# Convolution bias moved to VectorE, first expert pairs loaded earlier, a fill moved among the pairs

## The reference, cut to what matters

```python
x = x + _L0_conv_ref(_ln_c(x), ...)          # gating, 3x3 attention, product with gus, 1x1 product
t = t + _L0_ffn_ref(_ln_t(t), ...)           # 8 experts, each token goes to its best 2
x = x + _L1_conv_ref(_ln_c(x), codebook, bias)   # depthwise 7x7, out + bias[None, :, None, None]
t = t + _L1_ffn_ref(_ln_t(t), ...)           # 8 experts, best 2, with a capacity per expert
```

## Time and profile before

| | us |
|---|---|
| median of 3 runs | 2272.59 |
| lowest, highest | 2270.89, 2274.28 |
| the profiled execution's own time | 2273.36 |
| its span, first to last instruction | 2271.6 |
| TensorE busy | 1646.8 (72%) |
| VectorE busy | 1095.9 (48%) |
| GpSimd busy | 1023.3 (45%) |
| ScalarE busy | 697.3 (31%) |
| DMA, mean over the span | 122 GB/s |

### The profile page before, as it was taken

How to read it: one execution, slowest core, us unless ns; L and a number is a source line. 1 busy time by engine, 2 the same in 40 slices (tenths; PEclk the granted TensorE clock), 3 DMA queues, 4 the chain that set the end, 5 groups by cost and what they waited for, 6 DMA issues and landing times.

```text
span 2271.6 us, 34896 instructions
## 1 busy us (share of the span) xinstructions
PE 1646.8 (72%) x9963; PEld 1386.0 (61%) x9963; DVE 1095.9 (48%) x4024; ACT 697.3 (31%) x1433; POOL 1023.3 (45%) x1041
## 2 busy tenths in 40 slices
PE   4899996998559999999999908870000029999944
PEld 3777775776549999899988808870000016666632
DVE  3465557655555445677678872285000002222257
ACT  0323322232124444555555511030000014444412
POOL 2000004442357777767544470017777745554520
PEclk9999998999779999999999958985555559999965
DMA  3165544653866665998789445601110012232258
GB/s 114 49 113 77 103 90 98 140 104 74 131 149 179 182 181 166 232 240 233 201 211 234 149 107 113 125 21 51 55 51 25 4 25 77 80 88 77 79 190 272
DMA packets 325342, 277.62 MB, mean 122 GB/s; under 512 B 72514, under 2 KB 301655, under 8 KB 325051
## 3 DMA queue, kind: packets, MB, share of 16 engines
q1 hardware_dynamic: 259898, 207.65, 38.6%
q0 software_dynamic: 31488, 55.94, 7.6%
q10 hardware_dynamic: 33792, 12.06, 2.0%
HBM read 167.37 MB, written 109.43 MB: 122 GB/s over the span
## 4 chain that ended last, share of the span: by engine, by line
PE 54%; DMA 15%; DVE 13%; issue 7%; POOL 6%; ACT 3%; SPq 1%; DVEq 1%; POOLq 0%; ACTq 0%
PE zp L708 8%; DMA slots_cap<-arena 7%; PE tp L865 7%; PE zp L984 6%; POOL slots_cap L596 5%; PE tp L875 4%; PE gp L887 3%; PE zp L887 3%; PE tp L997 3%; DMA out<-arena 3%; PE tp L790 2%; PE zp L875 2%; PE gp L805 2%; DMA slots<-arena 2%; DVE arena L1674 2%
## 5 line engine op out<-in xcount | busy, mean ns | idle before, releaser
L596 POOL DMA_INDIRECT slots<-arena x256 | 252.9, 988 | 550.7 <-DVE arena L1459 376.8
L636 POOL DMA_INDIRECT results<-arena x304 | 301.1, 990 | 188.3 <-DVE arena L1519 110.3
L596 POOL DMA_INDIRECT slots_cap<-arena x256 | 251.6, 983 | 228.1 <-issue 184.8
L708 PE MATMUL zp<-arena 128*128 128x256 f32 x1024 | 242.9, 392 | 45.9 <-ACT arena L1038 45.6
L977 PE MATMUL gp<-arena 128*128 128x128 f32 x160 | 26.6, 289 | 306.7 <-DVE arena L1674 306.7
L708 PEld LDWEIGHTS zp<-arena 128*128 128x128 f32 x1024 | 197.6, 196 | 76.3 <-ACT arena L1038 47.9
L671 POOL DMA_INDIRECT results<-arena x160 | 158.9, 993 | 170.8 <-DVE arena L1689 132.1
L977 PEld LDWEIGHTS gp<-arena 128*128 128x128 f32 x160 | 17.4, 143 | 340.5 <-issue 303.2
L865 PE MATMUL tp<-arena 128*128 128x256 f32 x912 | 223.7, 382 | 0.5 <-issue 0.5
L1534 DVE SCALAR_TENSOR_TENSOR arena<-tp,arena 128x256 f32<-128x256 f32 x304 | 134.8, 481 | 131.5 <-PE tp L875 110.8
L865 PEld LDWEIGHTS tp<-arena 128*128 128x128 f32 x912 | 162.8, 192 | 16.9 <-issue 0.9
(11 more groups left out here) (257 smaller groups left out, 3268.9 us busy)
## 6 DMA issues: line engine op xcount, KB each, us to landing
arena<-in_L_ffn_W SPq DMA_DIRECT2D x304, 192.0 KB
arena<-results SPq DMA_DIRECT2D x56, 512.0 KB, 5.1
arena<-slots SPq DMA_DIRECT2D x152, 134.0 KB
arena<-taps SPq DMA_DIRECT2D x64, 224.0 KB, 4.6
slots_cap<-arena SPq DMA_DIRECT2D x20, 536.0 KB
arena<-slots_cap SPq DMA_DIRECT2D x40, 268.0 KB, 2.9
arena<-in_x SPq DMA_DIRECT2D x8, 1024.0 KB, 8.7
arena<-arena SPq DMA_DIRECT2D x128, 64.0 KB
```

The lines of the kernel that those rows point to most:

```text
L596: g.indirect_dma_start(slots[m], bass.IndirectOffsetOnAxis(ap=slot[:, k, blk:blk + 1].bitcast(U32), axis=0), rows[:, blk, :], None, bounds ...
L636: g.indirect_dma_start(results, bass.IndirectOffsetOnAxis(ap=row_at[:, q:q + 1].bitcast(U32), axis=0), y_tiles[:, q, :], None, bounds_chec ...
L708: t.matmul(dst, wg[:, j, k, :], xs[c][:, :, k, 0:P], start=(k == 0), stop=False)
```

## The change

Three edits. (1) GpSimd no longer adds the bias. VectorE, in place of two sums per PSUM bank, runs eight `scalar_tensor_tensor` per bank, one for each channel and half, which add the bank, the channel's bias and `xt`. (2) SP, after the last visit, waits for the last product (`z_ready`) instead of `lg_ready`, loads the weights of pair 0, the tiles of pairs 0 to 3 and the weights of pairs 1 to 3, and only then waits for `lg_ready` and loads `m2_s` and `b3_s`. (3) The two fills of the third table, until now in visits 8 and 9 of the mixer, are issued behind the weights of pairs 6 and 20.

```diff
@@ SP: fills
-                     **{i: (1, part * (i - 4), part) for i in range(4, 8)},
-                     8: (2, 0, G_PAIRS[2]), 9: (2, G_PAIRS[2], G_PAIRS[2])}
+                     **{i: (1, part * (i - 4), part) for i in range(4, 8)}}
@@ SP: after the pipeline
-            sp.wait_ge(sem("lg_ready"), PAIRS)
-            sp.dma_start(m2_s, moe_w2.rearrange("e (c f) d -> f e c d", f=P)).then_inc(sem("moe_in"), 16)
-            sp.dma_start(b3_s, moe_b3.rearrange("e (c f) -> f e c", f=P), allow_slow_non_contiguous=True
-                         ).then_inc(sem("moe_in"), 16)
+            def load_second():
+                sp.wait_ge(sem("lg_ready"), PAIRS)
+                sp.dma_start(m2_s, moe_w2.rearrange("e (c f) d -> f e c d", f=P)).then_inc(sem("moe_in"), 16)
+                sp.dma_start(b3_s, moe_b3.rearrange("e (c f) -> f e c", f=P), allow_slow_non_contiguous=True
+                             ).then_inc(sem("moe_in"), 16)
...
+            sp.wait_ge(sem("z_ready"), 8 * PAIRS)
             sp.wait_ge(sem("slots_ready"), 1)
-            for T in range(PT):
-                load_weights(T)
+            load_weights(0)
             all_sent(1)
             for T in range(PT):
                 load_pair(T, 0, T)
+            for T in range(1, PT):
+                load_weights(T)
+            load_second()
...
                 load_pair(T, g, n)
                 sp.wait_ge(sem("g_end"), T - PT + 1)
                 load_weights(T)
+                if T in (6, 20):
+                    fill_slots(2, G_PAIRS[2] * (6, 20).index(T), G_PAIRS[2])
@@ GpSimd
-            pool.wait_ge(sem("convb_in"), 16)
-            def add_bias(n, chunks):
-                alone("xn3_ready", chunks)
-                part = xt[:, bass.ds(KB * n, KB), :]
-                g.tensor_tensor(part, part, conv_b.rearrange("p (a c) -> p a c", a=1).to_broadcast([P, KB, P]), ALU.add
-                                ).then_inc(sem("biased"), 1)
-            with pool.Fori(0, CHUNKS // 2) as n:
-                add_bias(n, 2 * n + 2)
-            with pool.Fori(CHUNKS // 2, NBLK // KB) as n:
-                add_bias(n, n + CHUNKS // 2 + 1)
@@ VectorE
-            dve.wait_ge(sem("biased"), NBLK // KB)
+            dve.wait_ge(sem("convb_in"), 16)
+            dve.wait_ge(sem("xn3_ready"), CHUNKS + TAIL)
             with dve.Fori(0, NCG // 4) as turn:
                 for n in range(8):
                     dve.wait_ge(sem("conv_done"), 8 * turn + n + 1)
                     for h in range(2):
                         half = slice(NBLK // 2 * h, NBLK // 2 * (h + 1))
                         other = slice(NBLK // 2 * (1 - h), NBLK // 2 * (2 - h))
-                        at = xt[:, half, bass.ds(32 * turn + 4 * n, 4)]
-                        last = v.tensor_tensor(at, at, banks[n].rearrange("p (c k) -> p k c", c=4)[:, other, :], ALU.add)
+                        for c in range(4):
+                            chan = bass.ds(32 * turn + 4 * n + c, 1)
+                            at = xt[:, half, chan].rearrange("p k c -> p (k c)")
+                            last = v.scalar_tensor_tensor(out=at, in0=banks[n].rearrange("p (c k) -> p c k", c=4)[:, c, other],
+                                                          scalar=conv_b[:, chan], in1=at, op0=ALU.add, op1=ALU.add)
                     last.then_inc(sem("x3_ready"), 1)
```

## The result

The changed kernel takes 2286.78 us (median of 6 runs, 2283.18 to 2292.63), the kernel before on the same chip 2271.74 (6 runs, 2267.82 to 2274.28). The ratio is 1.0069, with a 95% interval of 1.0053 to 1.0086: 0.7% slower. Forecast were 2280 in a range of 2266 to 2288. The profiled run took 2287.52 with a span of 2285.8, so 14.2 more than the span of before.

A forecast was written before the change was run, and what follows sets the result against it. TensorE was taken to bound the expert pairs (54% of the span), so only its idle gaps could change. Tail -20.3, convolution +2.2, start -8.7 and fills +34.6 gave +7.8, so 2280 us on the median, range 2266 to 2288.

The forecast's parts named there:

- The fills: Expert pairs: tiles issued behind each moved fill wait for it, stalling pairs 7 and 21 by 17.3 us each, 34.6 together.
- Rival one: Expert pairs: tiles overtake the fill or the queue shares its engines, leaving only -26.8, so 2246 us; chance 0.08.
- Rival two: Expert pairs: the fill goes as fast as the idle 14.2 us row, stalls 11 to 12 us each, 2269; chance 0.27.
- The tail: Before the convolution: without GpSimd's bias adds VectorE's chain is shorter, the convolution 20.3 us earlier; bounds 16 to 20.
- Rival four: Tail: GpSimd is not what slows L90 to L96, and the bias does not pay, so 2298; chance 0.03.
- The start: First expert pair: early loads leave TensorE waiting only for b3; first transpose 9.2 us earlier, net 8.7 (7.7 to 9.2).
- The convolution: Bias on VectorE: eight instructions 0.2 us apart, 0.85 us more a bank, seen at the turns' waits; 2.2 us (0.6 to 4).
- The sign named for this term: Convolution: if VectorE's new instructions are over 0.33 us apart, the convolution term is wrong.
- Rival three: Convolution: VectorE becomes the bound from 0.335 us per instruction on; at 0.42 the whole comes to 2300; chance 0.04.
- the +2 to +13: Whole kernel: the span in which the forecast's net change lies, in us; the forecast keeps a chance of 0.58.

The follow-up runs named there:

- fill_act_queue: The changed kernel with the same two whole fills issued by ScalarE in its own queue, at its pairs 3 and 17: 2256.28 us, ratio 0.9941 to the kernel before.
- split_fill: The changed kernel with the two fills cut into 20 of 4 rows, one at each of pairs 6 to 25: 2251.80 us, ratio 0.9930 to the kernel before.
- bias_only: The kernel before with only the bias moved from GpSimd to VectorE, eight instructions a bank: 2261.98 us against 2271.19, ratio 0.9964.
- start_only_again: The kernel before with only the early loads of the first pairs, run a second time, on a chip like the first: 2267.29 us against 2268.53, ratio 1.0001.
- bias_left_out: The changed kernel without the convolution's bias, with the two VectorE sums per bank of before: 2276.43 us, ratio 1.0039 to the kernel before.
- best: split_fill with the bias added by VectorE in one 512-element instruction ahead of each bank's wait, then two sums: 2243.31 us, ratio 0.9898 to the kernel before.
- best_pool_add: best plus a one-column GpSimd sum that computes nothing used: 2236.68 us, ratio 0.9866 to the kernel before.
- no_bias_edit: The changed kernel with the bias back on GpSimd and two VectorE instructions a bank: 2294.30 us, ratio 1.0107 to the kernel before.
- fill_only: The kernel before with only the two fills moved behind the weights of pairs 6 and 20: 2299.71 us, ratio 1.0128.
- four_fills: The changed kernel with the fills cut into four of 20 rows, at pairs 6, 13, 20 and 27, on another chip: 2377.72 us against 2398.04, ratio 0.9902.
- after_pool_add: The changed kernel plus a one-column GpSimd sum that computes nothing used, on another chip: ratio 0.9993 to the kernel before.

## Why the prediction was right, and where it was off

**The fills: right.** Expected were 17.3 us each, 34.6 together; measured 17.7 and 17.1. The parts held as well. For the tile of pair 7 25.5 us from its issue were assumed; it was used 25.7 us after it (665.29 to 690.97), and the fills landed 26.0 and 25.6 us after theirs. From ScalarE's start on the tile to the next step 5.2 plus 1.2 for the clock, 6.05 measured (690.97 to 697.02). What the prediction didn't separate is that most of this is the place in the queue, not bandwidth: fill_act_queue moves the same bytes for 9.6 us, split_fill for none. Rival one falls with it: the tile did not overtake the fill. The Trainium skill, "DMA: Bandwidth & Descriptors", section on queues, rings and completion order, has descriptors consumed in ring order, with later writes free to finish first. Of its two halves the first decides here: the tile was used 0.2 us after the fill's landing. Rival two falls too: a fill beside the pairs' traffic lands as one beside the sends did, not in 14.2 us.

**The tail: right**, 20.3 forecast and 20.3 measured, the same in bias_only. Rival four falls. Its bounds of 16 to 20 left out the term itself, a slip that changes nothing. That small steps of 16 elements took as long as a GpSimd sum fits the Trainium skill, "SBUF — State Buffer", section "Who interferes with whom": VectorE's instructions with two SBUF inputs and GpSimd's reads share a port, held exclusively for an instruction. L93 and L96, with one tensor input, were as slow beside the sums (2.07 and 2.09 us), and that sentence does not cover them. The runs show the contention and its end; which port it was no run here shows.

**The start: right in size**, 8.7 forecast, 8.0 measured by pair 4, and b3 is what TensorE waits for. (The other early starts on these chips give 7.0 to 11.7 us at pair 4.) The reason given was incomplete. "The bursts of sends on GpSimd lose the fills beside them; nothing waits for them before pair 56, so nothing" fails: start_only_again has an equally early start and loses 7.3 us at pair 7, because the results stand behind the sends on GpSimd. In the whole change both edits come together, so the sum did not suffer.

**The convolution: mis-sized.** This is the term that failed: forecast 2.2 (0.6 to 4), measured 7.5, and 6.4 by bias_left_out. Two steps of it were off. First, the instruction: 0.2 us apart assumed, by taking 0.07 off the row of 128 elements; measured 0.234, which is 0.03 under the 0.26 of that row. No row gave the 0.07; halving the length saved half of that. The last of the eight also lasts 0.33, not 0.2. A bank costs 1.97 us instead of 1.6, 1.22 more than before where 0.85 were assumed, and the wait after the first turn grew by just that (1.07 to 2.30). The Trainium skill, "VectorE: DVE Perf Modes", section on the TRN2 errata, gives 184 cycles for it, an estimate of 192 ns; the trace has 234 from start to start. Its advice against many small tiles was the better guide: the 512-element form in best removes the cost. Second, the clock. The waits themselves grew by 3.8 us, and the taps did hide about half of it in the two inner turns, as assumed (1.85 to 2.30 and 1.45 to 2.30). But the prediction counted waits only: it put the clock after them at nothing. TensorE's products after the longer waits ran at 1.2 GHz for a while, and the same products took 3.3 us more, in the second turn (1.3) and the fourth (1.7) above all. The prediction had charged just this after the long stall among the pairs, and not here. The sign named for this term, over 0.33 us apart, was not seen, and the term was wrong all the same. Rival three falls: VectorE is not the bound, it still idles 0.7 us or more between banks.

**What was not in the sum.** The part behind the convolution takes 3.35 us more; the prediction had no term for it. GpSimd's sends are 8 ns longer each: from the first send into the last table to the last one the delay grows by 1.7 us, and from there to the last of the second layer's results by 1.45. The runs show that this goes with edit 1, though not by what means. From the last bank to the last stretch, the five profiles on these chips with a GpSimd sum in the program take 713.6 to 714.5 us, the six without one 715.3 to 718.0; the sends alone take 328.0 to 328.4 and 329.9 to 330.2. So a program without a GpSimd sum loses time behind the convolution: 1.7 us between best_pool_add and best, which differ in that sum alone, and some 3 us between the groups. This is part of why edit 1 alone brings less than tail and convolution together. Between pair 62 and the tail 3.2 us come back. Other kernels show -3.9 (best_pool_add) to +1.5 (no_bias_edit) from there to pair 151, so this may be a difference from run to run; no run settles it.

In all: forecast +7.8, measured +14.2 by the profiles and +15.0 by the medians. Of the 6.4 between forecast and profiles 5.3 are the convolution, 3.35 the last third, 0.9 the start and the fills, and -3.2 the late pairs. The direction was right because the fills' term was, the largest of the four. That the time lies in the range is in part luck: it is 1.2 us under the upper end and outside the +2 to +13 that the chances name for the forecast, and the 3.2 us that nothing foresaw kept it there. The upper end itself was added up too low: with the bounds given for the four terms (40 for the fills, 4 for the convolution, 16 and 7.7 for the gains) it would be 2293.

## What to carry to other kernels

Before a large transfer is moved to "where there is time", look at what stands behind it in the same queue: a 2.7 MB fill that held up nothing urgent in one place cost 17 us in another, nothing when cut into ten pieces of 268 KB, one to a pair, and 5 us from another engine's queue. An edit whose early start only pays when another queue is drained in time must be judged with that other edit, and a wait on TensorE should be priced with the clock it may lose afterwards, which here nearly doubled it. To fold an extra term into an accumulation, prefer one long instruction ahead of the wait to many short ones behind it.

## What the runs showed that was not expected

SP's issue of a transfer of 134 KB took 13.13 and 14.31 us behind the two fills (13.05 behind the first in fill_only) and 0.38 where the fill was in another queue. The kernel before had a case of it: of its two fills issued together at 585.3, the issue of the second took 17.06 us, where nothing urgent stood behind. So an issue behind a large transfer can hold the issuing engine, and all it would do next; that the queue was full is the reading, not shown.

GpSimd's indirect transfers take 0.982 us in the six profiles of programs that hold no GpSimd sum (the changed kernel, bias_only, split_fill, fill_act_queue, bias_left_out, best) and 0.972 to 0.974 in those that hold one, even of one column (best_pool_add). The same holds on the other chip (0.985 in four_fills, 0.974 in after_pool_add). Between best and best_pool_add, on one chip, the medians are 6.6 us apart and the runs don't overlap (2240.01 to 2244.23, 2235.64 to 2238.59), though the profiled spans differ by 1.4 only. What in the program does it is open.

The other chip takes 2398 us for the kernel that takes 2270 here. Its fills are slower (2412 KB land after 23.5 us in after_pool_add and 20.5 in the changed kernel here, the same code), its loads of 512 KB of results are not (5.3 and 5.5), and many pairs take 5.6 us instead of 4.15. A part that runs at TensorE's pace on one chip need not do so on another.
